# Attention and feed-forward block on Trainium2: tokens transposed in a second input and centred on GpSimd, weights by casting DMAs

## The reference

```python
# x: [16, 2048, 1024]
h   = ln(x)                                   # outer normalisation
n   = ln(h) * norm_w + norm_b
q, k, v = (n @ qkv_w.T + qkv_b) split by features, 1024 each
w   = softmax(q^T k / sqrt(2048), axis=keys)  # 1024 x 1024: over features, summed over tokens
a   = w @ v^T                                 # back to tokens x 1024
x1  = x + (a @ proj_w.T + proj_b + h)
z2  = ln(x1)
h1  = round8(z2 @ w1 + b1)                    # 4096 wide, multiples of 2^-8
h2  = round8(gelu interpolated between 33 points)
y   = x1 + (h2 @ w2 + b2) rounded to multiples of 2^-8
```

## Time and profile before

| what | us |
|---|---|
| median of 3 runs | 1382.72 |
| lowest and highest run | 1358.85, 1549.2 |
| profiled execution | 1362.81 |
| its span on the slowest core (core 1) | 1361.3 |
| TensorE busy | 1316.5 |
| VectorE, ScalarE, GpSimd busy | 1036.3, 805.4, 597.6 |
| attention part, to the start of the feed-forward part | 455 |

### The profile page before, as it was taken

The page is one execution under the profiler, slowest core; times in us unless marked ns, Lnnn a source line. Parts: engine busy times, 40 slices in busy tenths (PEclk is TensorE's granted clock), DMA queues, the critical chain, the costliest instruction groups (busy, mean ns, idle before and its releaser), DMA issues.

```text
span 1361.3 us, 22093 instructions; the slowest of 8 cores (1349.2 to 1361.3 us)
## 1 busy us (share of the span) xinstructions
PE 1316.5 (97%) x6232; PEld 596.2 (44%) x6232; DVE 1036.3 (76%) x1668; ACT 805.4 (59%) x1295; POOL 597.6 (44%) x443
## 2 busy tenths in 40 slices
PE   7998999999989997999999999999999999999998
PEld 3443454444434432444444444444444444444443
DVE  7366555735227788898898998898899889889884
ACT  6433544623126787766667666666667666666761
POOL 4820463513466665443434444444444444444440
PEclk9999999999999999999999999999999999999999
DMA  9999866599999870210120030031021012002003
GB/s 297 325 213 201 258 208 213 217 213 267 266 336 322 228 127 1 63 55 32 36 89 16 29 104 25 16 93 47 17 70 56 31 39 86 17 28 73 25 16 108
DMA packets 124539, 165.63 MB, mean 122 GB/s; under 512 B 74620, under 2 KB 74620, under 8 KB 124420
## 3 DMA queue, kind: packets, MB, share of 16 engines
q1 hardware_dynamic: 120964, 157.94, 39.5%
q0 software_dynamic: 3456, 6.29, 3.3%
HBM read 103.38 MB, written 50.33 MB: 113 GB/s over the span
## 4 chain that ended last, share of the span: by engine, by line
PE 78%; DMA 7%; issue 4%; ACT 4%; SPq 4%; DVE 2%; POOL 1%; ACTq 0%; DVEq 0%; POOLq 0%
PE pf L624 29%; PE pf L654 16%; PE pf L639 15%; PE pf L512 8%; PE pf L377 5%; DMA ring<-w_h 4%; SPq L253 2%; PE pf L461 2%; PE pf L406 1%; PE pf L501 1%; ACT gb L1134 1%; SPq L258 1%; DVE rbits L967 1%; ACT kb L1124 1%; DMA ring<-wv_h 1%
## 5 line engine op out<-in xcount | busy, mean ns | idle before, releaser
L1293 POOL TENSOR_TENSOR gb<-gb,ga 128x512 f32<-128x512 f32 x256 | 368.0, 1438 | 490.5 <-ACT gb L1134 490.5
L967 DVE SCALAR_TENSOR_TENSOR rbits<-ga,gb 128x512 int32<-128x512 f32 x256 | 287.1, 1122 | 0.6
L1124 ACT ACTIVATE kb<-pf,b1x 128x512 int32<-128x512 f32 x256 | 174.9, 683 | 175.9 <-PE pf L624 175.4
L639 PE MATMUL pf<-w,yt 128*128 128x512 bf16 x1024 | 256.7, 379 | 14.8 <-ACT yt L1142 14.8
L654 PE MATMUL pf<-w,yt 128*128 128x512 bf16 x1024 | 252.5, 379 | 0.1
L624 PE MATMUL pf<-z2cmB,w 128*128 128x512 bf16 x1024 | 241.9, 379 | 0.0
L624 PE MATMUL pf<-z2cmA,w 128*128 128x512 bf16 x1024 | 240.6, 379 | 0.0
L962 DVE SCALAR_TENSOR_TENSOR gb<-rbits,gb 128x512 f32<-128x512 int32 x256 | 224.9, 878 | 0.1
L1133 ACT ACTIVATE ga<-kb 128x512 f32<-128x512 int32 x256 | 159.8, 624 | 91.5 <-DVE rbits L967 91.0
L952 DVE TENSOR_SCALAR rbits<-kb 128x512 int32<-128x512 int32 x256 | 116.0, 453 | 87.0 <-ACT kb L1124 85.4
L1134 ACT ACTIVATE gb<-kb,c 128x512 f32<-128x512 int32 x256 | 181.4, 709 | 0.0
(11 more groups left out here) (96 smaller groups left out, 1073.3 us busy)
## 6 DMA issues: line engine op xcount, KB each, us to landing
ring<-xs SPq DMA_DIRECT2D x48, 512.0 KB, 6.4
ring<-w_h SPq DMA_DIRECT2D x48, 512.0 KB, 8.5
x1scr<-xo SPq DMA_DIRECT2D x32, 512.0 KB, 3.4
xh<-x1scr SPq DMA_DIRECT2D x64, 256.0 KB, 2.6
ys<-xh SPq DMA_DIRECT2D x64, 256.0 KB, 2.0
xin<-xs SPq DMA_DIRECT2D x16, 512.0 KB, 13.3
zscr<-Z SPq DMA_DIRECT2D x32, 256.0 KB, 8.8
z2scr<-z2b SPq DMA_DIRECT2D x32, 256.0 KB, 2.9
```

The source lines that it names most:

```text
L639: mm = t.matmul(bank(tt), y_tile(c, ft, tt), w2[:, ft, 0:512], start=(ft == 0), stop=(ft == 31))
L967: v.scalar_tensor_tensor(out=rbits[n % 5][:], in0=ga[n % 3][:], scalar=256.0, in1=gb[n % 3][:], op0=ALU.mult, op1=ALU.add).then_inc(S["v_h ...
L1124: a.activation(out=kb[n % 3][:], in_=bank(h_bank(n)), func=AF.Identity, bias=b1x[:, n % 32:n % 32 + 1], scale=256.0).then_inc(S["a_k"], 1)
L1293: g_.tensor_tensor(out=gb[n % 3][:], in0=gb[n % 3][:], in1=ga[n % 3][:], op=ALU.subtract).then_inc(S["g_d"], 1)
```

## The change

The host passes a second copy of the input, transposed (`xt_h`: 2 x 1024 x 2048). `zt` is no longer the normalised token but the centred one: a ring tile of `xt_h` (128 features x 1024 tokens) less a row of token means, by one GpSimd instruction (`centre`). The means go out of SBUF into `mscr` and come back spread over 128 partitions (`mrow`, four rows of 1024 tokens). The token's scale `sr`, left out of `zt`, is put into the addition of the output stage (`x1_tile`). `zscr`, its stores and the transposed loads are gone.

All weights come by casting DMAs that GpSimd issues. The ring carries only tokens: transposed tiles T and x tiles X (to normalise) and O (residual), in the order of `RING_UNITS`. `bias_v` reads wv from its bf16 tile. The tokens of sequence 1 are normalised eight tiles in the M stage and eight in the N stage, by `N_TOKENS`; before, it was six and ten.

```diff
+N_TOKENS = [[24], [25, 26], [27], [28, 29], [30], [31], [], [], []]
+RING_UNITS = ([("T", 0, k) for k in range(8)] + [("X", 1, t) for t in range(16)]
+              + [("T", 0, 8), ("O", 0, 0), ("O", 0, 1), ("T", 0, 9), ("O", 0, 2)]
+              + [unit for i in range(6) for unit in (("O", 0, 3 + i), ("T", 0, 10 + i))]
+              + [("O", 0, m) for m in range(9, 16)]
+              + [("T", 1, k) for k in range(16)] + [("O", 1, m) for m in range(16)])
...
+    xt_h = din("xt_h", [2, D, TB])
...
-    zscr = nc.dram_tensor("zscr", [T, D], BF16, kind="Internal").ap()
+    mscr = nc.dram_tensor("mscr", [2, TB], F32, kind="Internal").ap()
...
+            def store_means(b):
+                s.wait_ge(S["v_st"], 16 * (b + 1))
+                s.dma_start(out=mscr[b].rearrange("(t p) -> p t", p=128), in_=mv[:, 16 * b:16 * (b + 1), 0],
+                            allow_slow_non_contiguous=True).then_inc(S["d_ms"], 16)
+
+            def load_mean_row(b, h):
+                s.wait_ge(S["d_ms"], 16 * (b + 1))
+                s.dma_start(out=mrow[2 * b + h][:],
+                            in_=mscr[b, 1024 * h:1024 * (h + 1)].partition_broadcast(128)
+                            ).then_inc(d_mrow[2 * b + h], 16)
...
-            for j in range(4):
-                load(U_WQ + j, wq_h[j])
...
+            s.wait_ge(d_wk[0], 64)
             s.dma_start(out=nbb[:], in_=nbb_h).then_inc(S["d_nbb"], 16)
-            for j in range(6):
-                load(U_WV + j, wv_h[j])
...
+            load_bias_rows()
+            store_means(0)
+            s.wait_ge(d_wv[0], 64)
             s.dma_start(out=rbb[:], in_=pbb_h).then_inc(S["d_pb"], 16)
-            s.wait_ge(S["a_wk"], 8)
-            s.wait_ge(S["d_zst"], 256)
-            load_zt(0, range(4))
...
+            load_mean_row(0, 0)
+            s.wait_ge(d_wv[1], 64)
+            for u in range(UNIT["X", 1, 6]):
+                load(u)
+            s.wait_ge(S["pe_s"], 8)
+            load_mean_row(0, 1)
+            for u in range(UNIT["X", 1, 6], UNIT["T", 0, 8] + 6):
+                load(u)
+            store_means(1)
...
-                v.tensor_tensor(out=xo[g % 4][:], in0=pf[:, 512 * pair:512 * pair + 1024], in1=xo[g % 4][:],
-                                op=ALU.add).then_inc(S["v_x1"], 1)
+                v.scalar_tensor_tensor(out=xo[g % 4][:], in0=pf[:, 512 * pair:512 * pair + 1024],
+                                       scalar=sr[:, g:g + 1], in1=xo[g % 4][:], op0=ALU.mult,
+                                       op1=ALU.add).then_inc(S["v_x1"], 1)
...
+            def centre(b, k):
+                u = UNIT["T", b, k]
+                h, j = k // 8, k % 8
+                if j == 0:
+                    g_.wait_ge(d_mrow[2 * b + h], 16)
+                    if b == 1:
+                        g_.wait_ge(S["pe_out"], 8 * (h + 1))
                 landed(g_, u)
-                g_.tensor_copy(out=dst, in_=ring[u % 6][:]).then_inc(S[sem], 1)
+                g_.tensor_tensor(out=zt[:, j, 1024 * h:1024 * (h + 1)], in0=ring[u % 6][:], in1=mrow[2 * b + h][:],
+                                 op=ALU.subtract).then_inc(S["g_zt"], 1)
...
+            def load_w2(k):
+                g_.dma_start(out=w2[:, k, :], in_=w2_h[k]).then_inc(d_w2[k // 4], 16)
...
+            for k in range(8):
+                centre(0, k)
             accumulate(1, range(15))
-            out_stage(0)
...
+            for m in range(1, 17):
+                scale_tile(m - 1)
+                if m + 2 < 16:
+                    add_row(0, m + 2)
+                if m < 7:
+                    centre(0, 9 + m)
+                if m == 11:
+                    g_.wait_ge(S["pe_g"], 24)
+                if m >= 11:
+                    load_w1(2 * (m - 11))
+                    load_w1(2 * (m - 11) + 1)
+            for k in range(16):
+                centre(1, k)
+                if k < 4:
+                    load_w1(12 + k)
+            g_.wait_ge(S["pe_mv"], 2)
+            for k in range(16, 24):
+                load_w1(k)
+            g_.wait_ge(S["pe_s"], 16)
+            for k in range(24, 32):
+                load_w1(k)
             g_.wait_ge(S["pe_m"], 32)
-            for k in range(16):
-                cast(w2[:, k, :], U_W2A + k, "g_w2")
-            out_stage(1)
...
+            for k in range(8):
+                load_w2(k)
+            g_.wait_ge(S["v_rb"], 4)
...
+            for m in range(1, 17):
+                scale_tile(15 + m)
+                if m + 2 < 16:
+                    add_row(1, m + 2)
+                load_w2(7 + m)
...
-                if n < 14:
+                if 6 <= n < 14:
                     load_w2(18 + n)
```

283 lines of the change are left out of this document (124 added, 159 removed).

## The result

The changed kernel took 1414.25 us (median of 6 runs), the kernel before 1371.26 beside it (6 runs): ratio 1.0405, 95% interval 1.0388 to 1.0423. That is slower by 4%, above the range (1346 to 1382) and outside the likeliest case.

A forecast was written before the change was run, and what follows sets the result against it. TensorE, busy 97% of the span, was taken as the bound, with savings only where it idles or clocks lower. 1362.8 - 17.6 + 4.5 + 3 + 1 + 5 + 1.5 = 1360.2 us; 8-in-10 range 1346 to 1382.

The forecast's parts named there:

- the likeliest case: Whole kernel: 1352 to 1372 us, gains about paid back by costs; chance 0.58.
- (b): Gram on the second sequence's Z: statistics done earlier, so TensorE's wait for Z goes; gain 5.1 us.
- (a): M-stage matmuls of wsm with pw: p weights land earlier, so TensorE's wait goes; gain 4.9 us.
- (c): Last output stage: x tiles come some 70 us earlier in the ring, ending ScalarE's wait for them; gain 7.6 us.
- the first softmax term: Softmax of the first sequence: wsm and the column product wait out GpSimd centrings; cost 4.5 us (0 to 9).
- acc "to come with 10 us to spare": TensorE's need of acc at 70 us: no wait, 10 us to spare; a wait would show the forecast wrong.
- back to back at 1.53 us each: Transfers of the 32 p loads: 49 us in all, p landed by 81 us, GpSimd through issuing at about 65.
- T1 of the second sequence, 1 us (0 to 5): First output stage's last steps: 12 w1 loads and 6 token tiles fall there; xo stores needed 15 us later; cost 1 us.
- The second softmax, 3 us (0 to 6): Softmax of the second sequence: wsm waits out the centring in progress, 1.4 us per tile, three wsm; cost 3 us.
- The last output stage and the FFN's start, 5 and 1.5 us: w2 loads delay stores in the last output stage, 5 us (0 to 14); late z2 landing delays FFN, 1.5 (0 to 5).
- head start of 7 us of transfers in flight: Last output stage: 7 us of transfers may be in flight before stores are late, so 12 less 7 gives 5.
- rival "transfer-bound last stage": Last output stage becomes bound by transfers, TensorE's xo waits on x1 stores; 1373.7 us, chance 0.15 (stalled form 0.04).

The follow-up runs named there:

- e7: The changed kernel with w2 tiles 8 to 15 loaded before the last output stage, 16 to 31 one by one in the FFN: 1.0241 of before.
- e5: The changed kernel with the edits of e1, e3 and e7 together: 1382.11 us, 1.0114 of before.
- e1: The changed kernel with means transposed by VectorE and stored as 128-byte rows: Gram and T1 70.3 us in place of 78.3; read by stages alone.
- e3: The changed kernel with sixteen w1 loads moved behind the matvecs of sequence 1: T1 of sequence 1 34.7 us in place of 52.7; stages alone.
- e9: e8 with the transposed-tile loads of sequence 1 held until twelve t1m evictions by ScalarE are done: 1.008 of before.
- e8: e5 with twelve w1 loads between the centrings of sequence 1 and w2 tiles 8 to 31 spread in the FFN: 1.0055 of before.
- e4: The changed kernel with w2 tiles 8 to 15 loaded before the last output stage, 16 to 23 after: stage 60.6 us (68.0), FFN 914.1.

## Why the prediction was wrong

**Gains, 17.6 us.** (b) came: Gram on Z in 7.1 us instead of 12.0, 4.5 us in the mean of the cores. (a) and (c) were the waits of one core, taken for those of all eight. In the kernel before only cores 1 and 3 waited for pw (M stage 32.7 and 32.9 us, 27.6 on the other six), so the end of that wait is worth 1.3 us in the mean, and in the changed kernel waits for wsm and mm_ stand in its place (29.3 us). (c): ScalarE waits for no x tile ahead of the last output stage any more (3.1 to 9.0 us before, on cores 0 to 3), but the stage shows it only in e7: 55.3 us for the last output stage against 58.9 is 3.6, not 7.6. Of the 12 us of the last section 9.4 are these three.

**The four-byte store.** The prediction names it only as the top of the range of the first softmax term, and held acc "to come with 10 us to spare" at 70. On core 2 it came at 79; and the wv tile that bias_v needs ahead of the t1m eviction, which held up cores 3 to 7, is not among its waits at all. Two steps failed: the store's own transfers stand in no sum, though behind it the profile shows 50 GB/s; and the loads were reckoned back to back at 1.53 us each, which has GpSimd through its issues at 65 us and p landed by 81, while in e5, where the means are stored as rows, GpSimd issues the last p load at 92. Measured: +6.5 us in this stage, and e1 takes 8 off. "No row shows it" should have led to a rival of its own, a store that holds up every transfer.

**The first softmax, 4.5 us (0 to 9).** Measured +5.5. Place and size were right, the size partly by luck: the cores range from 31.5 to 43.8 us, since on some of them few centrings met the softmax (on core 0 the first starts at 106.9, near its end), and "waits out the GpSimd instruction in progress" was too mild, since one waited out three here and others up to eight in later kernels.

**T1 of the second sequence, 1 us (0 to 5).** Measured +23.2; this is the step that decides the case. I had written that the xo stores are needed 15 us later and never asked how late the stores would land, nor named those of z2, which have two buffers where xo has four: it is for them that ScalarE stood ahead of the t1m eviction. 12 casting loads and 6 token tiles fall into the last steps of a stage whose transfers I had myself put at the limit, for the second sequence. The same sum (3.8 us of transfers in a step of 3.456, plus loads) was not made for the first. The stores then landed after 18 to 22 us. e3 takes 18 us away by moving 16 loads, and in e9, which also holds back the token loads, the stage is at 29.6 as before.

**The second softmax, 3 us (0 to 6).** Measured +2.1, with 7.5 centrings beside it where T1's lateness left fewer than the eleven of e9; its wsm instructions waited for the one in progress, as the prediction has it, and none took over 2.37 us. In e8 and e9 the same stage cost 9 and 16 us more than before, but those kernels put a w1 load ahead of each centring there, which the changed kernel does not: by these traces most of that cost is my edit's, and not one that the late T1 had hidden.

**The last output stage and the FFN's start, 5 and 1.5 us.** After the gain of 7.6 the forecast was 2.6 us less than before for the stage, and the measurement is 9.1 more. Against the stage without the loads (e7) they cost 12.7 us, within the range of 0 to 14 and well over the 5 I took. The sum without the head start of 7 us of transfers in flight gives 12, so this term is the one that the measurement does not bear out. The FFN lost 5.7 where the range ended at 5; its first 64 matmuls take 20.3 us on cores 0 to 3 (13.9 before, in e4 and in e7), and e7 gets all of it back. The rival "transfer-bound last stage" had its mechanism right, but at 1373.7 it still assumed T1 and the store at little cost.

**The range.** Its top, 1382, was to be all costs "at three quarters of their tops". The tops add up to 39 us; three quarters of them on 1345.2 give 1374, and all of them 1384. So even with every cost at its top the measured 1414 stays out of reach: what is missing lies above all in T1 of the second sequence, 23.2 where the top was 5.

Three of the four terms that failed are one omission: each transfer was priced where it is needed, not where it makes a store wait that something else needs.
